# Causal masks of transposed scores: from a TensorE matmul per head to a GpSimd select per step

## The reference

```
xm = layernorm(x) * (1 + sc_a) + sh_a
q, k, v = split(xm @ Wqkv)                       # 16 heads of 16
scores = einsum('bhqd,bhkd->bhqk', q, k) * 16 ** -0.5
scores = where(tril(ones), scores, -inf)         # causal
attn = softmax(scores);  out = einsum('bhqk,bhkd->bhqd', attn, v)
x = x + gate * (out @ Wproj + bproj)             # and then an MLP of 1024 with gelu
```

## Time and profile before

| | |
|---|---|
| median of 3 runs | 1468.91 us (1466.01 to 1469.76) |
| profiled execution, its own time | 1477.51 us |
| its span, first to last instruction | 1475.7 us |
| busy PE / DVE / ACT / POOL | 87% / 59% / 46% / 16% of the span |
| granted TensorE clock, mean | 0.925 |

### The profile page before, as it was taken

How to read it: one execution, slowest core, us unless ns; L and a number is a source line. 1 busy time by engine, 2 the same in 40 slices (tenths; PEclk the granted TensorE clock), 3 DMA queues, 4 the chain that set the end, 5 groups by cost and what they waited for, 6 DMA issues and landing times.

```text
span 1475.7 us, 19136 instructions
## 1 busy us (share of the span) xinstructions
PE 1288.3 (87%) x7052; PEld 614.3 (42%) x7052; DVE 866.4 (59%) x1739; ACT 676.6 (46%) x1328; POOL 230.4 (16%) x256
## 2 busy tenths in 40 slices
PE   6795979999889998999899989999899988995871
PEld 5343534444434543454444544354444542442211
DVE  2633367755876468746875487747775576425611
ACT  1061116465446445545556544545546545650360
POOL 3003000210112002300222003200221020202002
PEclk8597979999989999999999999999999999996685
DMA  6305030411514041501532061503341142014002
GB/s 171 113 16 130 1 84 18 106 27 16 124 32 114 2 104 51 131 1 21 134 78 55 4 136 28 118 2 70 84 103 30 16 117 53 2 16 122 1 1 52
DMA packets 57924, 91.61 MB, mean 62 GB/s; under 512 B 10622, under 2 KB 21470, under 8 KB 57830
## 3 DMA queue, kind: packets, MB, share of 16 engines
q1 hardware_dynamic: 56822, 89.57, 26.3%
q10 hardware_dynamic: 1008, 0.81, 0.2%
HBM read 25.46 MB, written 4.77 MB: 20 GB/s over the span
## 4 chain that ended last, share of the span: by engine, by line
PE 62%; DVE 17%; issue 6%; DMA 5%; ACT 4%; SPq 3%; POOL 1%; ACTq 0%; POOLq 0%; DVEq 0%
PE SX L808 11%; PE OP L783 11%; PE DN L865 10%; PE SC L795 10%; DVE MX L625 8%; PE DN L911 7%; PE DN L890 7%; DMA KS<-PART 2%; DMA OC<-OE 2%; DVE STAT L632 2%; ACT E L502 2%; SPq L386 2%; PE SX L811 2%; PE DN L878 1%; PE SC L798 1%
## 5 line engine op out<-in xcount | busy, mean ns | idle before, releaser
L625 DVE TENSOR_REDUCE MX<-SX 128x1 f32<-128x512 f32 (+3 forms) x1024 | 557.5, 585 | 297.4 <-PE SX L811 192.3
L502 ACT ACTIVATE E<-SC 128x512 f32<-128x512 f32 (+3 forms) x1024 | 469.6, 521 | 384.3 <-PE SC L795 194.1
L808 PE MATMUL SX<-KS,QS 96*128 96x512 bf16 (+3 forms) x1024 | 334.3, 370 | 81.9 <-DVE MX L625 70.4
L795 PE MATMUL SC<-QS,KS 99*128 99x512 bf16 (+3 forms) x1024 | 302.8, 356 | 20.1 <-ACT E L502 9.6
L783 PE MATMUL OP<-E,V 128*32 128x512 f32 (+3 forms) x2048 | 241.3, 544 | 1.1 <-ACT E L502 1.1
L795 PEld LDWEIGHTS SC<-QS,KS 99*128 99x128 bf16 x1024 | 98.7, 100 | 295.0 <-ACT E L502 181.4
L808 PEld LDWEIGHTS SX<-KS,QS 96*128 96x128 bf16 x1024 | 101.0, 101 | 228.3 <-DVE MX L625 159.9
L911 PE MATMUL DN<-XT,W 128*128 128x512 f32 x256 | 123.0, 606 | 2.7 <-ACT HID L544 1.8
L890 PE MATMUL DN<-XT,WQKV 128*128 128x512 f32 x256 | 119.4, 610 | 2.4 <-DVE X L686 1.3
L420 POOL TENSOR_TENSOR RSTD<-VE,HALF 128x4 f32<-128x4 f32 x32 | 32.5, 1017 | 545.5 <-DVE VE L637 545.5
L865 PE MATMUL DN<-W,HID 128*128 128x256 f32 x512 | 117.2, 382 | 0.0
(11 more groups left out here) (89 smaller groups left out, 984.2 us busy)
## 6 DMA issues: line engine op xcount, KB each, us to landing
QS<-PART SPq DMA_DIRECT2D x96, 256.0 KB, 5.3
KS<-PART SPq DMA_DIRECT2D x96, 256.0 KB, 7.6
OC<-OE SPq DMA_DIRECT2D x64, 128.0 KB
RB<-recip_sums SPq DMA_DIRECT2D x64, 128.0 KB, 2.6
XIN<-in_x SPq DMA_DIRECT2D x8, 512.0 KB, 9.5
ROW<-row_vectors SPq DMA_DIRECT2D x8, 512.0 KB, 3.8
out<-OUT SPq DMA_DIRECT2D x8, 512.0 KB, 2.9
W<-in_w SPq DMA_DIRECT2D x2, 1024.0 KB, 7.2
```

The source lines that it names most:

```text
L502: a.activation(E[:, at["step"].index() % 2, j, lo:T], SC[(4 * s + j) % 3][:, lo:T], ACT.Exp, scale=HD ** -0.5 if attend == 0 else 1.0)\
L625: v.reduce_max(MX[:, qt, h:h + 1], SX[at["scan"].index() % 2][:, 0:w], AX.X, negate=True)\
L795: ins = t_.matmul(SC[u % 3][:, lo:T], KS[attend][0:ALL_ROWS, h, kt * P:kt * P + P], QS[attend][0:ALL_ROWS, h, lo:T], start=True, stop=atte ...
L808: ins = t_.matmul(bank[:, 0:w], QS[layer][0:CUT_ROWS, h, qt * P:qt * P + P], KS[layer][0:CUT_ROWS, h, 0:w], start=True, stop=layer == 1)
```

## The change

The 512 matmuls with CAUSAL_T and that tile (with its two set-up instructions) go. The exponentials are taken of unmasked scores. For each attend step of layer 0, at its "p", POOL then runs one `affine_select` over the four diagonal blocks of E together (128 partitions, 4 heads x 128 columns): it keeps an element where the column is at or past the partition, and writes 0 elsewhere. It waits for the last exponential of the step (`exp_done`), and pv of the step waits for it (`masked_pool`). Order and buffers stay.

```
@@ -151,6 +151,7 @@
                 at["head"].n += 4
                 at["step"].n += 1
+                at["masked"].n += attend == 0
@@ -397,21 +398,30 @@
+            zero = g.to_reg(0.0)
+
             def work(at, kind, what, b):
+                if kind == "attend":
+                    s, attend, half = what
+                    if half and attend == 0:
+                        lo = P * (s % TT)
+                        block = E[:, at["step"].index() % 2, :, lo:lo + P]
+                        wait(pool, exp_done, at["head"].at(1, 4))
+                        g.affine_select(out=block, in_=block, compare_op=ALU.is_ge, fill=zero, base=0,
+                                        pattern=[[0, 4], [1, P]], channel_multiplier=-1)\
+                            .then_inc(masked_pool, 1)
+                    return
@@ -773,6 +783,8 @@
                 wait(pe, exp_done, at["head"].at())
+                if attend == 0:
+                    wait(pe, masked_pool, at["masked"].at())
@@ -793,9 +805,7 @@
                 ins = t_.matmul(SC[u % 3][:, lo:T], KS[attend][0:ALL_ROWS, h, kt * P:kt * P + P],
-                                QS[attend][0:ALL_ROWS, h, lo:T], start=True, stop=attend == 1)
-                if attend == 0:
-                    ins = t_.matmul(SC[u % 3][:, lo:lo + P], ID16[:], CAUSAL_T[:], start=False, stop=True)
+                                QS[attend][0:ALL_ROWS, h, lo:T], start=True, stop=True)
                 ins.then_inc(head_full, 1)
```

More of the change, by code:

```diff
@@ L97 @@
 COUNTS = ("dense", "res", "bias", "maxima", "max0", "max1", "hold", "pack", "sums", "scale", "rows0",
-          "rows1", "keep", "x_in", "close", "stack0", "stack1", "high", "low", "low1", "norm", "head", "step", "group",
+          "rows1", "keep", "x_in", "close", "stack0", "stack1", "high", "low", "low1", "norm", "head", "step", "masked", "group",
           "scan", "halves")
@@ L231, in two_layers @@
         CAUSAL = sb("CAUSAL", [P, P], BF16)
-        CAUSAL_T = sb("CAUSAL_T", [P, P], BF16)
         CT = sb("CT", [P, KT, B])
@@ L290, in two_layers @@
         row1_dma = sem("row1_dma")
+        masked_pool = sem("masked_pool")
         bias_pool = sem("bias_pool")
@@ L399, in _ @@
             g.memset(CAUSAL[:], 0.0).then_inc(consts, 1)
-            g.memset(CAUSAL_T[:], 0.0).then_inc(consts, 1)
-            pool.wait_ge(consts, 5)
+            pool.wait_ge(consts, 4)
             for m in (ID32, ID16):
@@ L407, in _ @@
                             pattern=[[-1, P]], channel_multiplier=1).then_inc(consts, 1)
-            g.affine_select(out=CAUSAL_T[:], in_=CAUSAL_T[:], compare_op=ALU.is_ge, fill=MASKED, base=0,
-                            pattern=[[1, P]], channel_multiplier=-1).then_inc(consts, 1)
             g.memset(V[0][:], 1.0).then_inc(consts, 1)
@@ L932 @@
 SILU_READY, FIRST_NORM_READY, NORMS_READY, ROWS_READY = 3, 7, 16, 19
-N_CONSTS = 11
+N_CONSTS = 9
 _SHAPE = (B, T, D)
```

## The result

The changed kernel takes 1567.52 us (median of 4 runs, 1561.79 to 1569.69), the kernel before 1469.34 beside it: 1.0678 times as long, 95% interval 1.0645 to 1.0710, or 98 us more. I had said slower by 69 us, 1538, with 1500 to 1580 as the range. Direction and places were right; the size was not, and two of the sum's smaller terms, the clock and the removal, are to blame.

The account below looks back on a forecast made before the run. It took PE, busy 87% of the span, to pace the kernel. Waits of 7 + 13 + 24 + 18 less 13 for the removal gave +49 us, the clock +20: 1468.9 + 69 = 1538 us, range 1500 to 1580.

Parts of the forecast that it names:

- the clock: PE's granted clock falling after 19 new idle spells: 20 us lost, bounds 0 and 36.
- the removal: 512 mask matmuls taken off PE: 13 us gained, bounds 7 and 28.
- The select: One POOL select of 128 x 512 float32: 0.61 us; pv no earlier than 0.75 us after the last exponential.
- Rival 2: The select is slow, near 1.17 us, and gaps that now fit don't: 1565 to 1580 us; 17%.
- step 6: Select queued on POOL behind the power of stat_a, pv late by 2.2 us in passes 1 to 6: 13 us.
- step 9: Select behind close1, itself behind step 8's select; pv 5.3 us late, 3.7 net in passes 2 to 6: 24 us.
- step 14: Select queued on POOL behind q0, pv 2.5 us late in passes 0 to 6: 18 us.
- short gaps: Steps where pv closely follows the last exponential: 13 us of lateness, some 6 hidden ahead of the KS scan, 7 left.
- The rule on the ports: DVE and POOL lock a shared port pair; later close1 blocks DVE's norm, an estimated 6 us, changing no term.
- Passes: Sign in the profile after: passes 2 to 6 take 170 to 176 us instead of 160 to 164.
- Rival 1: The waits come but the clock doesn't fall more: 1518 us; 25%.
- Rivals 3 and 4: PE doesn't pace a pass and makes up for stalls: 1456 us, 4%; the same half absorbed: 1480 to 1500, 8%.

Follow-up runs that it names:

- e8: The kernel before with its mask matmuls kept, plus 128 selects on a scratch buffer in POOL's queue that no pv waits for: 1494.9 us.
- E6: The kernel before, with close1's last operation on POOL (OUT + TMP) made to wait until DVE is through norm_a: 1454.4 us, ratio 0.9925.
- e1: The kernel before without mask matmuls or selects, no causal mask applied to the exponentials, their scale 0.01: 1464.2 us, ratio 0.9985.
- e12: The changed kernel with the 512 mask matmuls kept, so the mask is applied twice, run beside the changed kernel: 1553.6 us against 1567.6.
- e5: The changed kernel with 8, 18 and 8 extra matmuls ahead of pv of steps 6, 9 and 14, run while PE waits: 1535.8 us.

## Why the prediction was right, and where it was not

**The select.** Predicted 0.61 us between 0.29 and 1.17; it takes 0.64. From the earlier trace rows and this, each element more costs (641 - 292) / 384 = 0.91 ns; my line had 0.84. Pv follows the last exponential by 0.80 to 0.85 us, against 0.75, in step 1 of the later passes 0.92: 0.07 from the exponential to the select and 0.10 to 0.15 from the select to pv, in place of my guess of 0.14 for both. Rival 2 is out.

The Trainium skill's "GPSIMD Engine Reference" (section 7) gives 2.03 or, unrolled twice, 1.03 cycles per element. At the page's 1.2 GHz, 0.91 ns is an estimated 1.09 cycles, so the trace agrees with the lower one.

**The three places.** Each wait is where the order put it, and near the length that I had said:

| place | predicted, us | measured idle ahead of pv |
|---|---|---|
| step 6, passes 1 to 6 | 6 x 2.2 = 13 | 14.1 |
| step 9, passes 2 to 7 | 5 x 3.7 + 5.3 = 24 net | 26.2, less 5 x 1.56 that is gone: 18.4 |
| step 14, passes 0 to 6 | 7 x 2.5 = 18 | 18.0 |
| short gaps, all | 13 | 13.2 |
| of these not ahead of the scan that waits for KS | 7 | 7.0 |
| sum (without the 13) | 62 | 57.5 |

Step 9 is 3.5 us in passes 2, 4 and 6, not 5.3: PE came there late itself, at the lower clock after step 6, so that it had less left to wait for. That the 6 us ahead of the scan cost nothing is my argument; no run tested it, and PE's own waits for KS in the steady passes of before are 0.8 us in all.

**The rule on the ports** changed no term, as I had said, and holds: the norm of pass 4 took 5.82 us where the estimate by that rule was 6 (6.61 in two other passes), and 6.57 in e8. The four operations of the norm show how: in the changed kernel the shortest takes 0.41 us and the longest 2.49, as the next row has it, which is that of the norm alone in this stretch.

```profile
L682 DVE TENSOR_SCALAR XN<-XIN,MV,RSTD x4: 405/1582/2492, 778.1 to 783.2; 128x256 f32<-128x256 f32 x4
```

(Duration in ns: shortest, median, longest.) Between two GpSimd operations DVE gets one of its own through, and each of these then lasts as long as the GpSimd operation beside it. By the Trainium skill's "SBUF — State Buffer" ("SBUF: two separate sides") whichever starts first, a GpSimd operation or a DVE one of the kinds that contend with it, has the pair for its whole length. DVE's maxima, which read PSUM, took 0.69 and 0.68 us beside L475 as elsewhere. E6 puts that rule to use: 8 of its 11 us are waits that it took away. I used it to check a term and overlooked that it also speaks of a wait of the kernel before, the 1.56 us, which could be had back.

**The terms that were mis-sized: the clock, "bounds 0 and 36; I take 20", and with it "I take 13" for the removal.** Together they were +7 us in the sum. Measured, 98 - 58 = 40 us are left for both, as a remainder. These two terms are 33 us short and the waits 4 too high, which makes the 29 us between forecast and result. On its parts: the removal is worth 2 us by e1, where idle time and the clock take the rest, and is a loss of 14 in the changed kernel by e12. The clock is worth 32 us or more by e5. I reasoned that each of 19 new stalls costs at most one spell of 2.6 us as in the earlier trace rows and that some were paid already. In the trace all 15 in passes 2 to 6 were followed by the lower level, and most spells were longer than that of the earlier trace rows: 10.2, 13.7 and 10.2 us in pass 4, where 6.8 was my unit. And the 13 us that I took off as paid already came from a profile with 30 us more at the lower level than the same kernel had beside the experiments; the median, to which I added the sum, holds less of it. Nor did I see that the two terms are one. The mask matmuls that were taken out had been activity between stalls; without them the same stalls are followed by half as much again to twice the time at 1.2 GHz (146 and 133 against 88 and 71 us). The 36 us, made from the length of a spell in the kernel before, were no upper bound.

How the 40 us split between the length of the stalls and the matmuls that are missing is not settled: e12 gives 14 to the latter, the 26 that remain are not measured by themselves, and e5 covers parts of both.

**Passes**: said 170 to 176 us, came 174 to 177, short by the same term. **Rival 1** (clock no worse, 1518) falls by the granted clock, 0.872 to 0.884 in ten executions for 0.925 to 0.941, and by e5. **Rivals 3 and 4** (faster, or half absorbed) fall, since nothing made up for a stall: e8 loses 29 us even where no pv waits.

## What to carry to other kernels

Before moving work to an engine with room on average, write down what stands in its queue at each place where the result is waited for; here work moved at three places took off 95 us and left some 7, and the select's own 0.64 us made little. Price a stall of PE with the clock that follows it, and count removed matmuls as activity that is removed, not only as time. Before comparing clocks, look at those of all executions: the profiled one of the kernel before was no typical one. Look for a long GpSimd operation beside a DVE operation whose duration is twice the usual: one wait that kept them apart gave the only gain of this study that leaves the result as it is.

## What the hardware showed that I had not expected

- More matmuls made the program faster: 512 more of them 14 us, 34 more in each of the steady passes 32 us.
- The same idle time of PE, 2.4 us at step 14, was followed by 10.2 us at the lower clock in four of five steady passes of the changed kernel and by 6.8 in the fifth, and by 6.8 in all five with the mask matmuls kept, in both profiles of each.
- Two profiles of the changed kernel had 401 and 364 us at the lower clock and spans of 1567.4 and 1557.0 us, with idle times behind the selects within 1 us of each other (65.6 and 66.5).
- DVE's norm operations take 0.41 us alone and up to 2.49 beside a GpSimd operation; one of them gets in between two GpSimd operations, and is then held for the whole of the second.
